# One core, four gated layers: the last mixture's rows carry residual, gate and norm factors, and ScalarE evicts the value sums first in its step

## The reference

```
x = x + tanh(g_xattn[l]) * attention_l(layernorm(x), ctx, ctx)
x = x + tanh(g_ffn[l])   * ffn_l(layernorm(x))
```

```
logits = t @ switch_w + switch_b
route_prob = softmax(logits); routes = argmax(route_prob)
y = gelu_tanh(t @ w1[e] + b1[e]) @ w2[e] + b2[e]      # of the chosen expert e
out = y * max(route_prob)
```

## Time and profile before

| | us |
|---|---|
| three runs | 1059.7, 1058.42, 1056.05 (median 1058.42) |
| the profiled execution | 1058.71 |
| its span, first to last instruction | 1056.9 |
| busy in the span: TensorE, VectorE, ScalarE, GpSimd | 909.0, 727.5, 633.7, 631.3 |
| mean granted clock of TensorE | 0.956 of full speed |

### The profile page before, as it was taken

One profiled execution on the slowest core, in us unless ns is written; L12 is line 12 of the kernel. 1 busy time (PEld: TensorE's weight loads), 2 busy tenths in 40 slices (PEclk: granted clock), 3 DMA queues, 4 the chain that ended last, 5 costly groups with the idle time before them and its releaser, 6 DMA issues.

```text
span 1056.9 us, 21908 instructions
## 1 busy us (share of the span) xinstructions
PE 909.0 (86%) x7627; PEld 735.7 (70%) x7627; DVE 727.5 (69%) x1618; ACT 633.7 (60%) x1496; POOL 631.3 (60%) x706
## 2 busy tenths in 40 slices
PE   2788888899798998686899998999999988768993
PEld 1566666677798988455676776777777766558993
DVE  6899999373577576577799895555555568836674
ACT  2666776533565656677688775555555556444663
POOL 0466776637773373689878685444444466636753
PEclk9899999999899999998999999999999999868997
DMA  7980000001332341110000000000500000022334
GB/s 233 335 234 2 1 2 1 1 23 53 104 109 59 85 114 51 28 29 16 19 2 1 2 1 2 1 1 2 179 2 2 1 2 2 27 56 62 94 96 147
DMA packets 76846, 57.54 MB, mean 54 GB/s; under 512 B 13603, under 2 KB 69539, under 8 KB 76548
## 3 DMA queue, kind: packets, MB, share of 16 engines
q1 hardware_dynamic: 70148, 42.59, 14.3%
q0 software_dynamic: 6592, 13.58, 4.2%
HBM read 35.30 MB, written 24.08 MB: 56 GB/s over the span
## 4 chain that ended last, share of the span: by engine, by line
PE 51%; POOL 18%; DVE 11%; issue 10%; ACT 8%; DMA 2%; DVEq 0%; SPq 0%; POOLq 0%; ACTq 0%
PE psS L1209 9%; PE psO L1826 5%; PE psS L1818 5%; PE psO L1219 5%; PE psT L1763 5%; PE psS L1219 4%; PE psS L1752 3%; POOL ring L2155 3%; POOL sorted_x L1439 3%; POOL xrows L1414 3%; PE psO L1777 3%; POOL ring L847 2%; PE psO L1784 2%; ACT oTs L1925 1%; POOL sorted_z L1452 1%
## 5 line engine op out<-in xcount | busy, mean ns | idle before, releaser
L2155 POOL TENSOR_TENSOR ring<-ring,mx 128x1024 f32<-128x1024 f32 x94 | 178.3, 1904 | 104.4 <-DVE mx L2032 104.2
L1913 ACT ACTIVATE pT<-psT 128x512 f32<-128x512 f32 x192 | 114.7, 597 | 163.0 <-PE psT L1763 163.0
L1266 ACT ACTIVATE pT<-psS,b1copy 128x128 f32<-128x128 f32 x468 | 133.7, 368 | 84.2 <-PE psS L1209 84.2
L1763 PE MATMUL psT<-ident,ring 128*128 128x128 f32 x768 | 125.1, 287 | 26.8 <-POOL ring L2155 19.9
L1209 PE MATMUL psS<-ring 128*128 128x128 f32 x936 | 130.7, 285 | 13.8 <-DVE ring L1324 7.9
L1763 PEld LDWEIGHTS psT<-ident,ring 128*128 128x128 f32 x768 | 87.5, 145 | 67.6 <-issue 25.5
L1209 PEld LDWEIGHTS psS<-ring 128*128 128x128 f32 x936 | 119.5, 200 | 17.0 <-issue 8.0
L2024 DVE TENSOR_TENSOR ring<-psS,bias 128x1024 f32<-128x1024 f32 x96 | 112.6, 1215 | 10.0 <-PE psS L1752 8.3
L2032 DVE TENSOR_REDUCE mx<-ring 128x16 f32<-128x1024 f32 x96 | 112.1, 1208 | 0.0
L1321 DVE COPY ring<-w 128x512 f32 x117 | 54.4, 465 | 57.9 <-PE psO L1219 31.5
L1414 POOL DMA_INDIRECT xrows<-sorted_y,rows x64 | 61.8, 965 | 51.0 <-DMA sorted_y<-pT 33.1
(11 more groups left out here) (304 smaller groups left out, 2076.4 us busy)
## 6 DMA issues: line engine op xcount, KB each, us to landing
w<-w_dram SPq DMA_DIRECT2D x34, 256.0 KB, 5.8
sorted_x<-late SPq DMA_DIRECT2D x18, 256.0 KB, 3.6
ring<-sorted_x SPq DMA_DIRECT2D x18, 256.0 KB, 3.5
sorted_y<-pT SPq DMA_DIRECT2D x17, 256.0 KB, 2.5
sorted_z<-blank_dram SPq DMA_DIRECT2D x2, 1584.0 KB, 10.2
ring<-sorted_z SPq DMA_DIRECT2D x12, 256.0 KB
xrows<-token_y SPq DMA_DIRECT2D x8, 256.0 KB, 3.5
ctxz<-ctxz_dram SPq DMA_DIRECT2D x1, 1056.0 KB, 5.6
```

The costliest lines, as they stand in the source:

```text
L1266: op = nc.scalar.activation(hs[:, j % 2, f, :], psS[:, j % 2, f * P:(f + 1) * P], func, bias=b1copy[:, j % 4, f:f + 1])
L1763: mm = nc.tensor.transpose(psT[:, i * P:(i + 1) * P], ring[:, u % NS, p * P:(p + 1) * P], ident[:])
L1913: nc.scalar.activation(pT[:, u % 2, 4 * h:4 * h + 4, :].rearrange("p a q -> p (a q)"), psT[:, :], ACT.Exp).then_inc(s_pT, 1)
L2155: nc.gpsimd.tensor_tensor(rows_, rows_, mx[:, u % 4, 0:NH].rearrange("p h -> p h ()").broadcast_to([P, NH, SK]), ALU.subtract).then_inc(s_ ...
```

## The change

Three things are changed.

1. `keep_outputs(n-1)` of ScalarE moves to the head of its step, ahead of `keep_probs(2n, 0)`.
2. What a row needs after the last mixture travels with it. The attention of layer 3 writes x into the first 128 columns of the rows to be scattered; behind them stand the row's number, its gate, and the scale and bias of its norm (copied there by ScalarE, 128x8 for a chunk). So the rows that are sorted are not normed ones. SyncE loads them, four columns wider, into the place of x and xnT, all six groups of a half at once; ScalarE normalises the tiles of the next group between the GELUs (two tiles behind each of the first two, and before the first group), the turn of the next group moves to the third tile; VectorE adds b2 and then, tile by tile, output times gate plus residual; GpSimd scatters the sum straight to `out` by the row's number. `token_y`, `ids`, `outputs_of`, `combine_last` and the store of x are gone.
3. The gates are worked out before ranking, since they must stand in the rows that are scattered: exp(z) is taken as (1 + tanh(z/2)) / (1 - tanh(z/2)). ScalarE takes one tanh, VectorE six or seven steps, at step RANK_AT for half 0 and behind the copies of the first tiles for half 1. The subtraction of the largest logit moves from the end of `place_rows` to that of `choose`. The exponential and the three steps at the end of the stream, and those at the end of the kernel, are gone.

```diff
@@ last_moe_sync
-            def load(g):
-                if g > 1:
-                    sp_.wait_ge(*q.xgt(g - 1))
-                sp_.dma_start(xg[:, g % 2]..., sorted_z[g // n][..., 0:D]...).then_inc(s_xl[1][g % 2], 16)
...
             for h in range(2):
                 sp_.wait_ge(s_sc[1][h], HT * 16)
...
+                for k in range(n):
+                    at, size = k * CH, group_size(1, h * n + k)
+                    sp_.dma_start(xz[h][:, at:at + size, :], sorted_z[h][at * P:(at + size) * P, :].rearrange("(t p) d -> p t d", p=P)).then_inc(s_zl[h][min(k, 2)], 16)
+            for k in range(YS):
+                sp_.wait_ge(s_ys[k], scattered(k, 2 * n))
@@ route_parts, choose
+                step(nc.vector.tensor_tensor(pr, pr, over(m), ALU.subtract))
+            def gates():
+                dve.wait_ge(s_gates[1], h + 1)
+                step(nc.vector.tensor_scalar(tmp, pr, -1.0, 1.0, ALU.mult, ALU.add))
+                step(nc.vector.reciprocal(tmp, tmp))
+                step(nc.vector.scalar_tensor_tensor(tmp, pr, 1.0, tmp, ALU.add, ALU.mult))
+                step(nc.vector.tensor_reduce(sm, tmp, AXX, ALU.add))
+                step(nc.vector.reciprocal(sm, sm))
...
+                        step(nc.vector.tensor_scalar(rows_[:, a - low:b - low, D + 1], sm[:, a - at:b - at], tg[:, LAYERS + 3:LAYERS + 4], None, ALU.mult))
@@ gates_scalar
-            nc.scalar.activation(rt3[h][:, 0], rt3[h][:, 0], ACT.Exp).then_inc(s_gates[1], 1)
+            nc.scalar.activation(rt3[h][:, 0], rt3[h][:, 0], ACT.Tanh, scale=0.5).then_inc(s_gates[1], 1)
@@ moe_scalar
+                for t in tiles:
+                    op = nc.scalar.activation(xg[:, g % 2, t * P:(t + 1) * P], rows_[:, t, 0:D], ACT.Identity, bias=rows_[:, t, D + 3:D + 4], scale=rows_[:, t, D + 2:D + 3])
...
                     gelu(j)
+                    if r and g + 1 < GROUPS[r] and t < turn_at(r, g):
+                        size = group_size(r, g + 1)
+                        norm_group(g + 1, range(t * 2, min(t * 2 + 2, size)) if turn_at(r, g) == 2 else range(size))
...
+                    if r and j == GATES_TILE:
+                        gates_scalar(act, 1)
-                    if t == 1 and g + 1 < GROUPS[r]:
+                    if t == turn_at(r, g) and g + 1 < GROUPS[r]:
                         evac_group(g + 1)
@@ moe_vector
-        def combine_last(dve, h, cc):
...
+            def add_residual(g, t, y):
+                loaded, rows_ = sorted_group(g)
+                dve.wait_ge(*loaded)
+                return nc.vector.scalar_tensor_tensor(y, y, rows_[:, t, D + 1:D + 2], rows_[:, t, 0:D], ALU.mult, ALU.add)
...
+                    for t in range(n):
+                        op = add_residual(g, t, y[:, t * P:(t + 1) * P])
+                    op.then_inc(q.ye.sem, 1)
...
+                if r and g == 0:
+                    second_gates()
                 outputs(g)
                 if r and g == 0:
                     rank_second()
@@ last_experts_gpsimd
-                    nc.gpsimd.indirect_dma_start(token_y[g // n], ...
+                    nc.gpsimd.indirect_dma_start(out, bass.IndirectOffsetOnAxis(rows_[:, t, D:D + 1].bitcast(I32), 0),
@@ stream_scalar
+                if 0 <= n - 1 < NB:
+                    keep_outputs(n - 1)
                 if 0 <= n < NB:
                     keep_probs(2 * n, 0)
                 if 0 <= n + AHEAD < NB:
                     keep_queries(n + AHEAD)
-                if 0 <= n - 1 < NB:
-                    keep_outputs(n - 1)
...
+                if n == RANK_AT:
+                    gates_scalar(act, 0)
...
-                if n == NB + 2:
-                    gates_scalar(act, 0)
@@ stream_scalar, normalise
+                    nc.scalar.activation(rows_[:, at:at + CH, D + 2:D + 4], lnrb[:, :, k, :].rearrange("p o t -> p t o"), ACT.Copy)
@@ stream_vector
+                to = xt if l < LAYERS - 1 else last_rows(QT * b, QT)
...
                 if n == RANK_AT:
+                    gates()
                     rank()
```

More of the change, by code:

```diff
@@ L1078, in choose @@
                 assert done[0] == CHOSEN
+                step(nc.vector.tensor_tensor(pr, pr, over(m), ALU.subtract))
+                assert done[0] == LOWERED
+            def gates():
[5 more added lines that the diff above has]
+                step(nc.vector.reciprocal(sm, sm))
+                dve.wait_ge(s_token, 2)
+                at = h * HT
+                for rows_, low, high in ((rows_low, 0, LOW * CH), (rows_high, LOW * CH, NT)):
+                    a, b = max(at, low), min(at + HT, high)
+                    if a < b:
+                        step(nc.vector.tensor_scalar(rows_[:, a - low:b - low, D + 1], sm[:, a - at:b - at], tg[:, LAYERS + 3:LAYERS + 4], None, ALU.mult))
+                assert done[0] == GATED[h]
             def rank():
@@ L1112, in place_rows @@
                 step(nc.vector.tensor_copy(expert[:, h * n:(h + 1) * n], expf[:, h * n:(h + 1) * n]))
[L1113 to L1122 removed]
+            return choose, gates, rank, place_rows
         def gates_scalar(act, h):
[L1125 to L1126 removed]
+            act.wait_ge(s_half[h], LOWERED)
+            nc.scalar.activation(rt3[h][:, 0], rt3[h][:, 0], ACT.Tanh, scale=0.5).then_inc(s_gates[1], 1)
         def shared_tensor(pe):
@@ L1267, in gelu, with norm_group @@
                 op.then_inc(q.act.sem, 1)
+            def norm_group(g, tiles):
+                loaded, rows_ = sorted_group(g)
+                if tiles[0] == 0:
+                    act.wait_ge(*loaded)
+                    if g > 1:
+                        act.wait_ge(*q.xgt(g - 1))
+                for t in tiles:
+                    op = nc.scalar.activation(xg[:, g % 2, t * P:(t + 1) * P], rows_[:, t, 0:D], ACT.Identity, bias=rows_[:, t, D + 3:D + 4], scale=rows_[:, t, D + 2:D + 3])
+                if tiles[-1] == group_size(1, g) - 1:
+                    op.then_inc(s_zn, 1)
+            if r:
+                norm_group(0, range(CH))
             evac_group(0)
@@ L1384, in moe_vector @@
                     rank_second()
-            if r:
-                second_gates()
-                for cc in range(NC // 2):
-                    combine_last(dve, 1, cc)
         def penalties(pool):
@@ L2142, in stream_vector @@
                     place_rows()
-                if n == NB + 3:
-                    gates()
             def take_last():
```

143 lines of the change are left out of this document (60 added, 83 removed).

## The result

| | before | after |
|---|---|---|
| median of 12 runs each, us | 1057.78 (1053.18 to 1060.37) | 1054.93 (1051.68 to 1057.61) |
| ratio of after to before | | 0.9964, 95% interval 0.9948 to 0.998 |
| the profiled execution, us | 1058.71 | 1056.08 |
| its span | 1056.9 | 1054.3 |
| mean granted clock of TensorE | 0.956 | 0.961 |

The change is worth 3.8 us by the ratio (2.1 to 5.5), not 12.6. The time lies just above the predicted range (1039 to 1054).

A forecast was written before the change was run, and what follows sets the result against it. No single bound: TensorE in the full stage and after 971 us, TensorE and VectorE close from 534 to 630, a chain without TensorE at the end. Terms -10.8, -7.2, -1.5, -0.5, +3.0, +4.1, +0.3 sum to -12.6: 1046.1 us, range 1039 to 1054.

The forecast's parts named there:

- The tail: End of the kernel: loads, additions and stores after the last scatter go, residuals come; -10.8 us (-12.2 to -9.5).
- the full stage: Attention stream, 630 to 843 us: evicting the value sums first saves 0.45 us in each of 16 steps; -7.2 us.
- The stage from 534 to 630: Twelve stream steps with the same TensorE wait, VectorE nearly full: evicting first gives -1.5 us (0 to -5.4).
- the other steps: Stream steps bound by GpSimd or VectorE: evicting the sums first gives -0.5 us.
- The bound of +2: Other stream steps: where ScalarE is late already, the eviction delays the probabilities by 0.5 us; bound +2 to -2.
- The rival that the eviction gives nothing: Stream: VectorE or GpSimd paces also where TensorE looks full; 1055.3 us, chance 0.10.
- Gates in the stream: Between choosing and ranking: seven VectorE instructions and a subtraction delay the load of the sorted rows; +3.0 us (+2.2 to +3.6).
- Head and first group: Start of the last mixture: normalisation after the load and more VectorE work before weight copies; +4.1 us (+3.0 to +7).
- the rest: Last mixture: ScalarE's normalisations between GELUs, narrowly hidden, and eight small copies of factors; +0.3 us (0 to +3).
- the prediction's own sign: First group of the last mixture: TensorE's stand before tiles 7 and 8 together 4 us longer.
- ScalarE didn't become the bound: Rival, last mixture: normalisations between GELUs make TensorE wait in every group; 1064 us in full, chance 0.05.
- No table was loaded for the tanh: Rival: second half's tanh between GELUs needs another table, two loads; 1048.7 us, or 1051.4 by the skill; chance 0.05.

The follow-up runs named there:

- e10: Changed kernel without GpSimd's drain, gates cheaper or moved off VectorE's critical stretches, sums' eviction put back behind the first probabilities in three steps; 1044.69 us, ratio 0.9867.
- e7b: Changed kernel without GpSimd's drain at the end of the block, run again on a chip like the first; 1047.66 us, ratio to before 0.9901.
- e1: Kernel before with only ScalarE's eviction of the value sums moved first in its step of the stream; 1054.36 us, ratio 0.9958.
- e5: Kernel before with one more GpSimd scatter after VectorE's last combining, rewriting the last tile's rows; 1062.02 us, ratio 1.0029.
- e4: Changed kernel with the last group's three tiles stored by SyncE as plain blocks, not scattered by GpSimd; 1050.32 us, ratio to before 0.9923.
- e2: Changed kernel with ScalarE's eviction of the value sums put back behind the first probabilities and queries; 1061.0 us, ratio to before 1.003.
- e3: Changed kernel with the first half's gates taken from the exponential, without three VectorE 128x128 operations; on another chip, ratio to before 0.9993.
- e6: Changed kernel with second half's gates and row placing moved to later tiles, group 1's outputs scattered before those rows; on another chip, ratio to before 1.0042.
- e7: Changed kernel without GpSimd's drain at the end of the block, on another chip; ratio to before 0.9952.
- e8: Kernel before without GpSimd's drain at the end of the block, on another chip; ratio 1.0014.

## Why the prediction was wrong, by its own steps

**The tail, -10.8 forecast, -5.2 measured.** The failed step is the one that let the end follow the last landing: "lands 2.3 later at 1045.9, and the end is 1046.1". The chain up to the last scatter was right: it was issued 2.0 us after TensorE's last matmul (1042.79 + 1.16 to 1045.99) for 1.0 us in before (1041.38 to 1042.42), so 1.0 later where 1.2 was forecast, and the scatters landed 2.2 us after their issue began, for 2.3. Nor did the copies beside it slow the issues: the last eleven took 0.95 or 0.96 us, so the trap "DVE blocks DMA" of the Trainium skill's "SBUF — State Buffer" had no part in it, as the prediction took it. What was left out is GpSimd's drain, which stood in the trace of before and ended 7.1 us after the last scatter, under the stores. By removing 12.2 us of work behind the scatter the change uncovered it. Without the drain the tail from the last matmul is 4.86 us for 15.52 before: -10.7. The size of the forecast was right for a kernel without a drain. For the stall in the full stage the prediction asked what is late next; for the end it didn't, and looked only at what was last in before, not at what ran beneath it.

**The stage from 534 to 630, -1.5, and the other steps, -0.5 forecast; +0.3 and +0.1 measured.** The first is the twelve steps up to 626.55 (92.03 us in before, 92.37 in after); the second is the steps ahead of them (+0.1), those behind the full stage (+0.3) and the way to the load (-0.2). The step that failed is taking a middle value between 0 and -5.4 for a stage that VectorE hands on. The light steps gave 0.05 us each. The bound of +2 for steps in which "ScalarE is late already, the eviction now delays the probabilities by 0.5" was the mechanism and the size (0.43 to 0.5, e10), but the sum didn't use it.

**The full stage, -7.2 forecast, -6.6 measured.** Right: steps of 13.41 us became 12.99, 0.42 less for 0.45. Nothing else was late next. The rival that the eviction gives nothing is out.

**Gates in the stream, +3.0 forecast, +3.5 measured.** The path named is there: GpSimd's wait for the maxima grew by 3.2 us, and TensorE, which the prediction left out, waits 2.23 us for the PSUM bank of the ranking. The reciprocal of 128x128, not in the trace of before, took 0.95 us as worked out from the two smaller ones. The term that was mis-sized is the first pass, 1.24 us for 0.29 beside GpSimd's subtraction; as the ranking's first product had paid 0.56 of this in before, some 0.4 of it is new, most of the difference.

Together these put the load 2.7 us earlier (net of the later start of the stream) where the prediction said 6.2.

**Head and first group, +4.1, and the rest, +0.3.** Load to last matmul is +1.6 in the pair of traces, but that pair isn't alike. Granted clock in the 40 us from the load (before; after; e7b, whose code is that of after up to here):

```profile
935.50:975.50 40.00, 31.19 (x217) 30.31 (x218) 22.77 (x89) 19.30 (x58) 15.92 (x17) 0.77 0.27 64
```

```profile
936.45:976.45 40.00, 28.12 (x209) 27.15 (x210) 26.20 (x100) 24.45 (x72) 13.74 (x15) 0.81 0.20 58
```

```profile
934.17:974.17 40.00, 28.22 (x198) 27.25 (x199) 24.86 (x96) 23.66 (x71) 13.27 (x14) 0.76 0.20 58
```

From the load to the last matmul these took 105.9, 107.5 and 108.8 us. Of the others, e1 and e5, with the last mixture of before, took 105.7 at 0.77 and 103.5 at 0.85; e4 and e2, with that of after, 107.5 at 0.81 and 110.4 at 0.72. Where both are alike in clock (0.76 and 0.77), the cost is 108.8 - 105.8 = 3.0 us; the plain means differ by 3.5; forecast were 4.4. By stretches, each start of a tile's `up` counted from the load:

| | tile 0 | tile 8 | tile 8 to 12 | tile 12 to the last matmul |
|---|---|---|---|---|
| before, e1, e5 | 6.0, 6.2, 6.2 | 29.4, 29.4, 28.3 | 10.6, 10.4, 9.3 | 65.9, 65.9, 65.9 |
| after, e4, e7b, e2 | 7.3, 7.3, 6.6, 6.8 | 33.2, 33.1, 33.1, 33.1 | 7.6, 7.7, 9.0, 10.6 | 66.7, 66.7, 66.7, 66.7 |

So up to tile 8 the forecast of +4.1 is borne out (+3.8 in the pair), and the rest costs 0.8 in every trace, for +0.3. What the prediction held for equal, or for longer in after, is the stretch behind. In before tile 8's eight matmuls still take 2.04 us, for 1.06 at the higher level of the clock; in after tile 7's take 1.76 and tile 8's 1.13. This stretch varies by 3 us among executions of the same code, and in three of these four it was shorter than in before. How the stand shows in after, to be set beside the earlier trace rows:

```profile
936.45 3.12 SPq L352 DMA_DIRECT2D x<-sorted_z  x6
...
943.70 2.08 PE L1209 MATMUL psS<-ring 128*128 128x128 f32 x8 [0.69 <-ACT ring L1259]
...
964.64 1.76 PE L1209 MATMUL psS<-ring 128*128 128x128 f32 x8 [4.23 <-DVE ring L1335]
...
969.61 1.13 PE L1209 MATMUL psS<-ring 128*128 128x128 f32 x8 [1.51 <-issue]
```

The first tile starts 7.25 us after the load for 5.96, 1.3 more (0.65 forecast, and 0.6 in e7b). The stand moved from tile 8 to tile 7: 4.23 and 1.51 us for 0.82 and 3.12, 1.8 us more, where the prediction's own sign asked for 4.

**The other rivals.** ScalarE didn't become the bound: 50.20 of 59 us and TensorE at 58.93. No table was loaded for the tanh (L1114) between the GELUs: after the load of 943.67 for the GELU there is none.

```profile
943.67 1.28 ACT L1266 ACT_TABLE_LOAD   x1
...
954.18 0.33 ACT L1114 ACTIVATE ctxz<-ctxz 128x128 f32<-128x128 f32 x1
```

The Trainium skill's "ScalarE: Activation LUTs", section on table sets, lists tanh with the exponential and left this open; here the table of this GELU holds it too.

**The sum.** Load -2.7, last mixture +3.0, tail -5.2: -4.9 us, inside the measured 2.1 to 5.5. With the plain means' 3.5 for the last mixture it is -4.4. Of the 7.7 us by which the forecast was too low 5.6 are the drain, 3.5 the stream, and the last mixture gave 1.4 back.

## What to carry to other kernels

Before taking work off the end of a kernel, list what every engine does behind its last instruction, the block's closing line included: what ends there under cover is the new end. An instruction moved ahead in a queue costs most of its length in the steps where that engine comes late (0.5 of 0.6 us here), and gains only where the one that waits for it is the bound, so judge it step by step. And compare two traces from marks that both have, since a head that runs the same code can start the rest several us apart.

## What the runs showed of the hardware

GpSimd's drain at the end of a block took until 6.9 to 7.2 us after its last indirect DMA was issued, in all eight traces that have one (before, after, e1, e2, e3 and e6 7.1, e4 6.9, e5 7.2), whether that DMA landed 2.2 or 3.9 us after its issue began. The drain's own length varied from 8.3 to 9.3 us. What it does in that time no row shows, and as the scatter was GpSimd's last instruction in all eight, neither is it shown that the time hangs on a DMA.

In six traces (after, e2, e4, e6, e7, e7b) the gates' first VectorE pass over 128x128 took 1.24 or 1.25 us instead of 0.29 and ended 0.08 or 0.09 us behind GpSimd's subtraction of 128x1024, beside which it had begun; in before and e1 the ranking's first product took 0.84 and ended 0.15 behind it. Not every instruction was held so: in e3 a reduction and a reciprocal of 16 took 0.27 and 0.25 beside it.

A power of 128x16 elements on GpSimd (e10) was slow, against 0.23 us for a product of the same shape (L1496):

```profile
948.33 2.91 POOL L1493 TENSOR_TENSOR rs<-rs,minus 128x16 f32<-128x16 f32 x1
```

On the other chip the kernel before took 1190.34 us for about 1058, with the stream's steps at the same 7.3 and 13.4 us. The 130 us lay in the two mixtures (100 in layer 0's and 40 in the last in e8's trace, a slower execution than most), for the most part in stands that come back at nearly the same places in its four traces, as this one of ScalarE in e8:

```profile
1092.06 1.14 ACT L1266 ACTIVATE pT<-psS,b1copy 128x128 f32<-128x128 f32 x4 [20.07 <-remote]
```

What it waited for there, the trace doesn't say, and it stays open.
